# A six-block decoder on one core: first keys and queries ahead of values, rotary rows flipped among the value projections, low-rank weights as 64 columns, one-head cross attention by token halves

## What is computed

```python
x = layernorm(x + L0_attn(x))           # A: 32 heads of 16, ALiBi, causal
x = layernorm(x + L0_xattn(x, ctx))     # B: 32 query heads, 8 key heads of 128, rotary, mask
x = layernorm(x + L0_ffn(x))            # C: dense + 8 low-rank experts, top 2
x = layernorm(x + L1_attn(x))           # D: 32 query heads, 8 key heads of 128, window of 64
x = layernorm(x + L1_xattn(x, ctx))     # E: one head over all 512 features
x = layernorm(x + L1_ffn(x))            # F: 4-bit weights with scales, low-rank terms of rank 32

def L1_xattn(text, features):
    Q = text @ Wq.T + bq
    K = features @ Wk.T + bk
    return softmax(Q @ K.T / sqrt(512)) @ features

def qlinear(x, q, scale, A, Bm):        # gate, up and down of F
    return x @ ((q - 7.5) * scale * 0.005).T + 0.02 * (x @ A @ Bm)
```

## Time and profile before

| what | value |
|---|---|
| median of three runs | 1708.49 us |
| the profiled execution, whole | 1707.01 us |
| its span, first to last instruction | 1705.2 us |
| mean granted TensorE clock | 0.979 |

### The profile page before, as it was taken

One profiled execution on the slowest core, in us unless ns is written; L12 is line 12 of the kernel. 1 busy time (PEld: TensorE's weight loads), 2 busy tenths in 40 slices (PEclk: granted clock), 3 DMA queues, 4 the chain that ended last, 5 costly groups with the idle time before them and its releaser, 6 DMA issues. The chain is left out here.

```text
span 1705.2 us, 22804 instructions
## 1 busy us (share of the span) xinstructions
PE 1596.9 (94%) x8526; PEld 1277.1 (75%) x8526; DVE 983.1 (58%) x1946; ACT 659.7 (39%) x1191; POOL 202.9 (12%) x146
## 2 busy tenths in 40 slices
PE   8788689999999999999889999999999999979998
PEld 6565477788778778876777788788878877757866
DVE  5897757756676676667433542552553446246645
ACT  4666424433443443334333332332332323336541
POOL 8421130000000000000340000000000000703330
PEclk9999899999999999999999999999999999999999
DMA  5110011100110110100111110110110100202221
GB/s 211 50 44 26 15 48 38 62 26 27 50 50 1 51 62 13 38 13 26 45 51 38 38 50 9 53 52 10 49 62 12 37 13 25 79 6 83 77 80 50
DMA packets 26023, 75.44 MB, mean 44 GB/s; under 512 B 3888, under 2 KB 4624, under 8 KB 25680
## 3 DMA queue, kind: packets, MB, share of 16 engines
q1 hardware_dynamic: 25552, 73.16, 12.9%
q0 software_dynamic: 384, 1.05, 0.2%
HBM read 72.10 MB, written 2.10 MB: 44 GB/s over the span
## 5 line engine op out<-in xcount | busy, mean ns | idle before, releaser
L83 PE MATMUL bankY<-sb_Dwo,sb_DoT 128*128 128x512 f32 x768 | 193.4, 401 | 0.3 <-DVE sb_DoT L1033 0.3
L83 PE MATMUL bankY<-sb_Bwo,sb_BoT 128*128 128x512 f32 x768 | 193.3, 401 | 0.2 <-DVE sb_BoT L1033 0.2
L83 PE MATMUL bankA<-sb_xT,sb_Bwq 128*128 128x512 f32 x768 | 190.1, 397 | 0.0
L83 PE MATMUL bankA<-sb_xT,sb_Dwq 128*128 128x512 f32 x768 | 189.9, 396 | 0.0
L83 PEld LDWEIGHTS bankY<-sb_Dwo,sb_DoT 128*128 128x128 f32 x768 | 140.6, 189 | 42.4 <-issue 13.6
L83 PEld LDWEIGHTS bankY<-sb_Bwo,sb_BoT 128*128 128x128 f32 x768 | 140.8, 189 | 42.1 <-issue 13.2
L83 PEld LDWEIGHTS bankA<-sb_xT,sb_Dwq 128*128 128x128 f32 x768 | 142.2, 188 | 34.1 <-issue 2.7
L83 PEld LDWEIGHTS bankA<-sb_xT,sb_Bwq 128*128 128x128 f32 x768 | 142.3, 188 | 33.7 <-issue 2.4
L964 DVE TENSOR_TENSOR sb_BqT<-bankA,sb_Btable 128x512 f32<-128x512 f32 x64 | 44.2, 691 | 151.6 <-ACT sb_Bsw L866 151.6
L1000 DVE TENSOR_TENSOR sb_xtok<-sb_xtok,bankY 128x512 f32<-128x512 f32 x128 | 87.1, 680 | 53.7 <-PE bankY L83 53.6
L866 ACT ACTIVATE sb_Bsw<-bankA 64x512 f32<-64x512 f32 x160 | 94.8, 593 | 54.8 <-PE bankA L83 51.7
(11 more groups left out here) (277 smaller groups left out, 2987.1 us busy)
## 6 DMA issues: line engine op xcount, KB each, us to landing
sb_raw<-in_w_attn SPq DMA_DIRECT2D x80, 512.0 KB, 3.4
sb_raw<-in_q_gu SPq DMA_DIRECT2D x22, 256.0 KB, 2.7
sb_raw<-in_q_d SPq DMA_DIRECT2D x11, 256.0 KB, 2.7
sb_rawx<-in_xT SPq DMA_DIRECT2D x4, 512.0 KB, 6.5
sb_raw<-in_wqk SPq DMA_DIRECT2D x8, 256.0 KB, 2.6
sb_xtok<-in_x_tok SPq DMA_DIRECT2D x1, 2048.0 KB, 11.9
sb_raw<-in_ctxT SPq DMA_DIRECT2D x4, 512.0 KB, 3.8
sb_raw<-in_ctx_tok SPq DMA_DIRECT2D x4, 512.0 KB, 3.8
```

The costliest lines, as they stand in the source:

```text
L83: last = nc.tensor.matmul(out, lhs, rhs, start=start and i == 0, stop=stop and i == len(pairs) - 1)
```

## The change

It does the following.

1. **Stage A.** SP loads the keys' and queries' blocks of chunk 0 first, each ahead of a chunk of `xT`; the value blocks follow. PE makes keys and queries of chunk 0 first, chunk by chunk in four banks (`kqbank`), then the values tile by tile in the two banks of `bankT`; the first three scores stand behind the values of tiles 3, 4 and 5. The value banks of tiles 0 to 3 are drained by DVE, those of tiles 4 to 7 by ACT. POOL's order becomes keys and queries 0, values, context 0 and 1, keys and queries 1, context 2, output weights; the first output block waits for all value products. DVE drains four tiles, runs the front of units 0 and 1 and the back of unit 0, and only then adds the output bias to the eight tiles. At the end the last `low_last` stands ahead of the last-but-one residual.
2. **Stage B.** Two tiles of rotary rows are flipped ahead of each of the four value projections, and on DVE the copies to the table stand between the three mask instructions.
3. **Stage E.** The pieces come by token half: keys and queries of the first half, then those of the second. The scores of the first half go to `bankO` behind piece 8, its softmax runs beside the pieces of the second half, and its four attention tiles stand between pieces 12, 13 and 14. The last load of stage D fetches the keys' weights instead of the queries'.
4. **Stage F.** `a_d` holds high and low side by side as 64 columns, so that one matmul with each part of `hT` replaces three; the product low by low is now included. ACT moves the low half down with the factor 0.02, DVE adds the high half, ACT copies the sum twice, DVE subtracts.

The core of the diff:

```diff
@@ stage A
+        kqbank = [bankY[0][:], bankY[1][:], bankO[:, 0, :], bankO[:, 1, :]]
-        order = [("v", k) for k in range(KC)] + [("qk", 0), ("qk", 1), ("c", 0), ("c", 1), ("c", 2), ("qk", 2), ("qk", 3), ("p", 0), ("p", 1)]
+        order = [("qk", 0), ("qk", 1)] + [("v", k) for k in range(KC)] + [("c", 0), ("c", 1), ("qk", 2), ("qk", 3), ("c", 2), ("p", 0), ("p", 1)]
...
                     elif kind == "p" and i == 0:
-                        pool.wait_ge(a_ready, NT)
+                        pool.wait_ge(a_ready, 4 + NT)
...
                 for k in range(KC):
-                    pe.wait_ge(w_low, k + 1)
                     pe.wait_ge(in_low, k + 1)
-                    for t in range(NT):
-                        done = product(vbank[t], three([w[:, k, t * P:(t + 1) * P] for w in xT], [w[:, k, :] for w in wbig]), start=k == 0, stop=k == KC - 1)
+                    for i in range(4):
+                        if k == 0 and i < 2:
+                            pe.wait_ge(w_low, order.index(("qk", i)) + 1)
+                        done = product(kqbank[i], three([w[:, i % 2, k, :] for w in wqk], [w[:, k, i // 2 * HALF:(i // 2 + 1) * HALF] for w in xT]), start=k == 0, stop=k == KC - 1)
...
+                def values(t):
+                    if t >= 2:
+                        v_drained(pe, t - 2)
+                    for k in range(KC):
+                        if t == 0:
+                            pe.wait_ge(w_low, order.index(("v", k)) + 1)
+                        done = product(bankT[t % 2][:], three([w[:, k, t * P:(t + 1) * P] for w in xT], [w[:, k, :] for w in wbig]), start=k == 0, stop=k == KC - 1)
+                    done.then_inc(a_ready, 1)
...
-                for i in range(4):
-                    project(0, i, range(KC))
-                pe.wait_ge(small, 112)
-                for n in range(AHEAD):
-                    scores(n)
+                for t in range(NT):
+                    values(t)
+                    if 3 <= t < 3 + AHEAD:
+                        scores(t - 3)
+                pe.wait_ge(small, 80)
...
+                for t in range(4):
+                    values(t)
+                in_turns(front(0))
+                in_turns(front(1), back(0))
                 dve.wait_ge(in_tok, 16)
                 for t in range(NT):
                     nc.vector.tensor_tensor(xtok[:, t, :], xtok[:, t, :], bp[:], ALU.add).then_inc(pbias, 1)
-                for t in range(0, NT, 2):
-                    values(t)
-                in_turns(front(0))
-                in_turns(front(1), back(0))
                 for n in range(UNITS):
...
-                    if n > LAST_CHUNK:
+                    if LAST_CHUNK < n < UNITS - 1:
                         residual(n - LAST_CHUNK - 1)
                 low_last(NT - 1)
+                residual(NT - 2)
                 residual(NT - 1)
@@ stage B
                         for x in START:
+                            if rope and x[0] == "V":
+                                flip(2 * x[1], 2 * x[1] + 1)
                             project(part, x)
...
+                        to_table(0, 1)
                         nc.vector.tensor_scalar(hidden[:], mask[:], 0, -1.0e9 * HD ** 0.5, ALU.is_equal, ALU.mult).then_inc(bounded, 1)
+                        to_table(2, 3)
                         nc.vector.tensor_scalar(bound[:], mask[:], 0, -OFF, ALU.not_equal, ALU.mult).then_inc(bounded, 1)
...
+                        to_table(4, 5)
                         dve.wait_ge(bounded, 2)
                         nc.vector.tensor_tensor(bound[:], bound[:], hidden[:], ALU.add).then_inc(bounded, 1)
+                        to_table(6, 7)
@@ stage E
+        PIECES = [(a, m, h) for h in range(2) for a in (1, 0) for m in range(KC)]
...
+                pieces(0, 1, 2, 3, 4, 5, 6, 7, 8)
+                scores(0)
+                pieces(9, 10, 11)
+                flip(0)
+                pieces(12)
+                attend(0, 1)
+                pieces(13)
+                attend(2, 3)
+                pieces(14, 15)
+                scores(1)
+                flip(1)
+                attend(4, 5, 6, 7)
@@ stage F
-                        done = product(bankA[h][0:LR_RANK, :], [x for i in ([NI - 1] if last else range(NI - 1)) for x in three([w[:, i, :] for w in a_d], [s[:, i, cols] for s in hT])],
+                        done = product(bankA[h][0:2 * LR_RANK, :], [(a_d[:, i].rearrange("p a n -> p (a n)"), s[:, i, cols]) for i in ([NI - 1] if last else range(NI - 1)) for s in hT],
                                        start=not last, stop=last)
...
+                    nc.scalar.activation(us[h][R0, :], bankA[h][R1, :], ACT.Copy, scale=LR).then_inc(d_moved, 1)
...
+                    act.wait_ge(d_sum, h + 1)
                     for dst in (R0, R2):
-                        nc.scalar.activation(stack[0][dst, cols], bankA[h][R0, :], ACT.Copy, scale=LR).then_inc(lr_high, 1)
+                        nc.scalar.activation(stack[0][dst, cols], us[h][R0, :], ACT.Copy).then_inc(lr_high, 1)
```

More of the change, by code:

```diff
@@ L392, in _ @@
                     else:
[L393 removed]
+                        v_drained(pe, NT - 2 + n)
                     for i in range(4):
@@ L727, in _, with flip @@
                     ln_tensor(pe, norm)
-                    if rope:
-                        pe.wait_ge(gathered, 16 * NT)
-                        for t in range(NT):
+                    def flip(*tiles):
+                        for t in tiles:
                             if t >= 2:
```

263 lines of the change are left out of this document (158 added, 105 removed).

## The result

The changed kernel takes 1691.51 us (median of four runs, 1690.22 to 1692.31), the kernel before beside it 1708.76. The ratio is 0.9898 with a 95% interval of 0.9884 to 0.9912, so the change gains 17.3 us (15.0 to 19.8). A second comparison, on another chip, gives 1687.60 against 1703.39, 15.8 less, and a ratio of 0.9901 (0.9885 to 0.9918), which is 16.9 (14.0 to 19.6). The forecast was 1696.0, a gain of 12.5. The direction and the range held; the gain was larger than forecast.

What follows compares the result with a forecast made beforehand. PE, busy 94% of the span, was taken to bound the kernel. The terms -9.5 (B), -2.5 (E), -3.5 (F) and +3.0 (A) sum to -12.5 us: 1708.5 to 1696.0, forecast 1691 to 1700 (0.60), wider range 1686 to 1703.

Steps and rivals of the forecast that it cites:

- Bound and places: Whole kernel: PE is busy 94% of the span, so time can come only from its matmuls or its waits.
- Stage B, -9.5: Stage B's start: flips among the value projections let keys start earlier, -9.5 us, with a thin DVE margin.
- Stage E, -2.5: Stage E in two token halves: PE's work is the same, the last softmax chain ends earlier, -2.5 us.
- Stage F, -3.5: Stage F: 22 fewer matmuls save 5.1, but down tiles wait for POOL's last conversion, so -3.5 us.
- Stage A, end, -2.0: End of stage A: the last low part ahead of the last-but-one residual brings the last residual earlier, -2.0 us.
- Stage A, start, +5.0: Start of stage A: DVE's additions stand behind POOL's splits and delay unit 1, costing 5.0 us; the least trusted term.
- The walk: Start of stage A: PE, POOL and DVE queues followed in time; unit 0 flipped at 47.8, unit 1 at 63.4.
- The slow unit: Stage A, behind PE's 12 us idle time: one unit takes 4.7 us in place of 3.2.
- From there the loops are the same: Stage A after unit 2: the loop runs as before, so the start's cost stays 5 us.
- Rival 1: Stage A's start: the additions hide from POOL's splits, giving -8.6 in place of +5.0, 1682.4 us; chance 0.15.
- Rival 3: Stage A's loop: DVE sets the pace and is slower, +21 us, 1717; chance 0.05.
- Rivals 2 and 4: 2: covers too short in B, E, F, A's start, 1700.6, chance 0.17; 4: B gives nothing, 1705.5, chance 0.03.

Runs made afterwards that it cites:

- The run by chunks: Changed kernel with POOL's splits spread out, stage E's attention tiles 2 and 3 later, F's first down tile waiting per weight chunk; ratio 0.9826, 1674.42 us.
- bias_loop: Changed kernel with the eight output-bias additions moved into stage A's loop on DVE, behind odd turns 5 to 19; ratio to before 0.9879.
- the best kernel: Changed kernel with E and F edits and long POOL splits behind units 3, 9, 19 and 23 of stage A; 1668.92 us, ratio 0.9777.

## Why the prediction was right, and where it was off

- **Bound and places.** PE bounds the kernel, and the time came out of its waits and matmuls where the working put it. Right.
- **Stage B, -9.5.** Keys were forecast at 19.4 behind the stage's start and came at 18.6 and 19.3; before they came at 29.0 and 28.7. That is -10.4 and -9.4 for -9.6. DVE followed with a thin margin as walked, and the run with the masks first shows how thin: without the new order of DVE 6 us are lost. In the changed kernel the copies for the third flips end 0.3 us before PE wants them.
- **Stage E, -2.5.** The second half's softmax was forecast at 62.1 behind the stage's start and began at 62.0, its first attention tile at 68.9 and came at 68.7. The stage is 1.7 to 2.2 shorter. Right within the bounds.
- **Stage F, -3.5.** POOL's last conversion did become the end, as forecast, but it ended 0.4 later in the stage than before (115.0 against 114.6). The stage is 3.1 shorter. The run by chunks took 1.6 to 1.9 more by removing that wait.
- **Stage A, end, -2.0.** From unit 31 on it measured -2.1, with the part undone as the counter-test.
- **Stage A, start, +5.0.** This term was mis-sized; its mechanism was right. (The +3.0 in the heading of its paragraph is the sum of both ends of the stage.) The additions were forecast to last 17.7 us from 42.5 on, and lasted 16.5 from 40.7 on. The 17.7 were 12.9 of POOL's instructions and 4.8 of the additions themselves. The 16.5 are 0.4 ahead of POOL's first instruction, 15.0 for its six, and 1.1 behind the last; the own time of the other additions lay beside POOL's instructions. So POOL's part was put 2.1 too low and the additions' 3.3 too high, and that the whole came out near is partly luck. The walk was also late by 1.8 us at once, since it let PE do the products with chunk 0 at half rate up to 14, and PE went over to its full rate near 11 (in the second trace near 12). That too is in part chance: in the other traces of this stage's start it was at 11.4 to 15.3. Unit 1 came at 60.3 for 63.4. The slow unit behind the wait took 5.7 instead of the 4.7 taken over from before. So unit 3 is late by 2.8 and 3.7 in the two pairs, not by 5. One more us comes back at unit 18, 4.85 us long for 5.90 before. "From there the loops are the same" was wrong by that. In both kernels PE has just waited 3.3 us there and works at the lower clock; in the changed one it rises sooner. It is not a price of the new order as such: the kernel with stage A's part alone has the same order, and its unit 18 takes 5.90, at a granted clock of 0.50 from 122.5 to 129.3. The windows before (window, length, busy time of PE, PEld, DVE, ACT and POOL, granted clock, DMA share, GB/s):

```profile
122.60:126.00 3.40, 3.40 (x9) 2.22 (x7) 3.40 (x7) 0.90 (x2) 0.00 (x0) 0.50 0.47 192
```

And after:

```profile
125.60:128.00 2.40, 2.40 (x8) 1.68 (x6) 2.40 (x5) 0.63 (x1) 0.00 (x0) 0.68 0.63 254
```

- **The sum.** With the measured terms it is +0.6 - 9.9 - 2.0 - 3.1 = -14.4, inside the forecast. The medians say -17.3 and -15.8 (by the ratios -17.4 and -16.9), with intervals that reach to -15.0 and -14.0, and the spans of the two pairs of traces -15.1 and -15.5. Between 1 and 3 us are therefore in no term. The time fell near the lower end of the 1691 to 1700 by a cheaper stage A and by this part, which may be in what varies between runs (the stop of ACT, the turns of stage B), of which a trace shows one case each; this stays open.
- **Rivals.** Rival 1, additions that hide, was wrong: they took 16.5 us. Rival 3, DVE setting the pace of the loop, did not happen, since the loop's units have their old lengths from unit 3 on; but bias_loop shows how near it was. Rivals 2 and 4 did not happen either.

## What to carry to other kernels

Before a block of DVE work on SBUF is moved, look at what POOL does in the new place: beside POOL's splits eight additions took 16.5 us, with POOL idle 4.9, in time that PE filled anyway. Moving POOL's optional work (what is needed much later) out of the way was worth more than the whole reordering of the stage: 204.8 became 188.6, where the reordering alone had left the stage, stops of ACT aside, as long as before within 1 us. In the best kernel the long splits were kept apart; that their distance is what matters was not tested by itself. And take a second trace of both kernels before a difference of 1 to 4 us between two traces is put down to the change.

## What the runs showed of the hardware that I had not expected

- A DVE instruction on 128x512 with a single SBUF input ran in 416 ns while POOL was idle, and took 2.1 to 2.6 us beside POOL's splits.
- ACT stood for 3.2 to 4.7 us with all its inputs there, in 3 of 12 traces, always in unit 25 of stage A, beside the gathers of the rotary rows. Its cause is not known; the profile calls it remote.
- At the program's start the first six matmuls take 2.93 us, half their later rate, and the granted clock reads 1.00 there. That 1.00 is no measurement: the trace of this kernel has its first record of the clock at 11.08, and the view shows 1.00 where there is none. In all 12 traces the first record stands within 0.15 us of the place where PE goes over to its full rate (11.2 here, 14.1 in the kernel before). Behind the wait of 11.45 us in stage A the rate is half as well, and there the granted clock reads 0.50, the lower level. The windows of the changed kernel, with columns as above:

```profile
8.00:11.00 3.00, 2.83 (x7) 2.21 (x8) 1.71 (x3) 2.33 (x3) 3.00 (x3) 1.00 0.98 358
...
60.30:62.50 2.20, 2.18 (x7) 1.91 (x8) 2.20 (x5) 0.88 (x3) 0.00 (x0) 0.50 0.00 0
```
